# Turning the second context chunk of a streamed attention before its loop, and the later chunks three steps ahead instead of two

## The reference, cut to what matters

```python
x = x + xattn(layernorm(x), ctx)     # x: (2, 512, 512), ctx: (2, 8192, 512)
x = x + ssm(layernorm(x))            # long convolution through a Fourier transform
x = x + ffn(layernorm(x))            # 8 experts, each token takes the best one
# inside xattn
h = history @ hW.T + hb;  c = combined @ cW.T + cb
q = h @ qW.T + qb;  k = c @ kW.T + kb;  v = c @ vW.T + vb
attn = softmax(q @ k.T / sqrt(512))
out  = (attn @ v + q) @ oW.T + ob
```

## Time and profile before

| | |
|---|---|
| time, median of 3 runs | 1181.11 us (1179.37 to 1183.04) |
| the profiled execution, its own time | 1183.38 us |
| its span, first to last instruction | 1181.6 us |
| TensorE busy | 1097.0 us, 93% |
| TensorE weight loads busy | 887.9 us, 75% |
| VectorE busy | 925.3 us, 78% |
| ScalarE busy | 515.1 us, 44% |
| GpSimd busy | 483.9 us, 41% |
| mean granted TensorE clock | 0.966 |

### The profile page before, as it was taken

One profiled execution on the slowest core, in us unless ns is written; L12 is line 12 of the kernel. 1 busy time (PEld: TensorE's weight loads), 2 busy tenths in 40 slices (PEclk: granted clock), 3 DMA queues, 4 the chain that ended last, 5 costly groups with the idle time before them and its releaser, 6 DMA issues.

```text
span 1181.6 us, 16713 instructions
## 1 busy us (share of the span) xinstructions
PE 1097.0 (93%) x4945; PEld 887.9 (75%) x4945; DVE 925.3 (78%) x1979; ACT 515.1 (44%) x1091; POOL 483.9 (41%) x432
## 2 busy tenths in 40 slices
PE   7999989999999999999899999999999999565497
PEld 5787868788888888788678888888888888453365
DVE  7952688898888888865489889899898675978584
ACT  4221165565555555443444444444444422423261
POOL 4702154354454454212244444444443316452353
PEclk9999989999999999999999999999999999877599
DMA  8210579888678676423367868878866510117691
GB/s 280 96 57 36 89 195 201 201 200 199 178 194 197 178 192 164 125 72 86 75 174 184 202 173 194 200 174 195 199 178 180 155 37 1 71 38 248 234 330 59
DMA packets 202198, 184.36 MB, mean 156 GB/s; under 512 B 18160, under 2 KB 147216, under 8 KB 202146
## 3 DMA queue, kind: packets, MB, share of 16 engines
q1 hardware_dynamic: 180930, 141.26, 47.8%
q10 hardware_dynamic: 17856, 32.51, 7.9%
q0 software_dynamic: 3360, 9.97, 2.3%
HBM read 142.77 MB, written 42.73 MB: 157 GB/s over the span
## 4 chain that ended last, share of the span: by engine, by line
PE 75%; DVE 12%; issue 4%; POOL 4%; DMA 3%; ACT 1%; SPq 0%; POOLq 0%; ACTq 0%; DVEq 0%
PE bank L563 37%; PE bank L702 27%; PE bank L908 3%; PE bank L782 2%; PE bank L751 2%; PE bank L571 1%; DMA zT<-in_L_ffn_expert_w_dram 1%; DVE h L1450 1%; PE bank L597 1%; DVE probs L1450 1%; DMA spectra<-mixed,gather_rows 1%; POOL rows L1985 1%; DVE h L1326 1%; DMA stage<-in_L_xattn_hW_dram 1%; POOL hl_F L1860 1%
## 5 line engine op out<-in xcount | busy, mean ns | idle before, releaser
L563 PE MATMUL bank<-hl_C,hl_D 128*128 128x512 f32 x768 | 189.0, 396 | 11.7 <-POOL hl_C L1867 11.7
L702 PE MATMUL bank<-hl_F,probsT 128*128 128x512 f32 x768 | 190.7, 397 | 0.3 <-DVE probsT L1525 0.2
L702 PE MATMUL bank<-hl_A,probsT 128*128 128x512 f32 x768 | 190.3, 396 | 0.0
L563 PE MATMUL bank<-hl_B,hl_D 128*128 128x512 f32 x768 | 184.6, 390 | 0.3 <-POOL hl_B L1867 0.2
L563 PEld LDWEIGHTS bank<-hl_C,hl_D 128*128 128x128 f32 x768 | 146.7, 191 | 44.8 <-POOL hl_C L1867 12.5
L1053 ACT ACTIVATE probs<-bank,nbias 128x512 f32<-128x512 f32 x128 | 88.2, 689 | 208.3 <-DVE nbias L1513 208.3
L1860 POOL TENSOR_TENSOR hl_A<-stage,hl_A 128x512 fp32r<-128x512 f32 x64 | 84.7, 1324 | 215.9 <-ACT hl_A L1020 215.8
L1860 POOL TENSOR_TENSOR hl_F<-stage,hl_F 128x512 fp32r<-128x512 f32 x64 | 85.4, 1334 | 210.3 <-ACT hl_F L1020 210.3
L702 PEld LDWEIGHTS bank<-hl_F,probsT 128*128 128x128 f32 x768 | 144.0, 188 | 35.4 <-POOL hl_F L1860 0.6
L702 PEld LDWEIGHTS bank<-hl_A,probsT 128*128 128x128 f32 x768 | 144.2, 188 | 34.2
L563 PEld LDWEIGHTS bank<-hl_B,hl_D 128*128 128x128 f32 x768 | 143.9, 188 | 32.7 <-issue 1.2
(11 more groups left out here) (401 smaller groups left out, 1853.9 us busy)
## 6 DMA issues: line engine op xcount, KB each, us to landing
p_rows<-probs ACTq DMA_DIRECT2D x124, 256.0 KB, 3.2
stage<-in_ctx_dram SPq DMA_DIRECT2D x112, 256.0 KB, 3.6
spectra<-in_ctx_dram SPq DMA_DIRECT2D x64, 256.0 KB, 5.4
xb<-in_ctx_dram SPq DMA_DIRECT2D x64, 256.0 KB, 5.2
resid<-p_rows SPq DMA_DIRECT2D x248, 64.0 KB, 2.2
stage<-in_L_ffn_expert_w_dram SPq DMA_DIRECT2D x9, 1024.0 KB, 8.3
h<-p_rows SPq DMA_DIRECT2D x124, 64.0 KB, 2.1
obB<-p_rows SPq DMA_DIRECT2D x124, 64.0 KB, 2.3
```

The lines of the kernel that those rows point to most:

```text
L563: last = nc.tensor.matmul(dst, lhs[:, a, t, k * P:(k + 1) * P], rhs[:, c, t, :], start=(t == 0 and (a, c) == PASSES[0]), stop=(t == T - 1 ...
L702: last = nc.tensor.matmul(obank[u % 2][:], probsT[u % 2][:, a, j, :], nat[b][par][:, c, j, :], start=(j == 0 and (a, c) == PASSES[0]), sto ...
```

## The change

VectorE turns three blocks of chunk 1 ahead of the loop (`second_chunk`), not two. For the first attention they come before the four additions into `xb` (L1409), not behind them. In the loop it turns a block three steps before it was due by count, not two (`TURNED_AHEAD`), and in the second attention the turning stands ahead of the four spectral products of the step, not behind. ScalarE and GpSimd take blocks 0, 1 and 2 of chunk 1 in step 0 and block 3 in step 1 (`FIRST_BLOCKS`), and GpSimd takes these ahead of the natural tile of the step. SyncE loads all four quarters of a later chunk in the step in which it loaded the first two; before, the other two came a step later.

```diff
+FIRST_BLOCKS = ((0, 1, 2), (3,), (), ())
+TURNED_AHEAD = 3
@@ SyncE
                     if n % T == T - 1:
-                        next_squares(b, n // T + 3, (0, 1))
-                    elif n % T == 0:
-                        next_squares(b, n // T + 2, (2, 3))
+                        next_squares(b, n // T + 3)
...
-            def next_squares(b, c, rows_of):
-                if 2 < c < NCH:
+            def next_squares(b, c):
+                if c < NCH:
                     sp.wait_ge(cT_split, b * BLOCKS + T * (c - 2))
-                    for j in rows_of:
-                        load_square_rows(b, c, j)
+                    load_squares(b, c)
@@ ScalarE
-                            for dd in BLOCKS_OF_STEP[u % T]:
+                            for dd in blocks_of(u, first):
                                 context_block(t, u, dd)
@@ VectorE
+            def second_chunk(b):
+                dve.wait_ge(in_squares[b][1], 16 * T)
+                for dd in range(TURNED_AHEAD):
+                    nc.vector.transpose(squares[b][1][:, dd], squares[b][1][:, dd]).then_inc(cT_ready, 1)
...
                 nc.vector.tensor_copy(ubB[:], bank_of("ubias")[:]).then_inc(evacuated, 1)
+                second_chunk(0)
                 for k in range(T):
                     add_to_x(f"qo1.{k}", 1, k)
...
-                    par, dd = ((u + 2) // T + 1) % 2, (u + 2) % T
+                    par, dd = ((u + TURNED_AHEAD) // T + 1) % 2, (u + TURNED_AHEAD) % T
...
+                        if not (first and u < 2):
+                            row_sums(*back(t, u, 2))
+                        if not (last and u + TURNED_AHEAD >= T):
+                            next_square(t, u)
                         if not kernel_terms and u % 3 != 2 and u < 7:
                             output_products(u - u // 3, t, t * P, P, small_parts)
-                        if not (first and u < 2):
-                            row_sums(*back(t, u, 2))
-                        if not (last and u + 2 >= T):
-                            next_square(t, u)
...
-                dve.wait_ge(in_squares[b][1], 16 * T)
-                for dd in range(2):
-                    nc.vector.transpose(squares[b][1][:, dd], squares[b][1][:, dd]).then_inc(cT_ready, 1)
...
                 first_lo(1)
+                second_chunk(1)
@@ GpSimd
+                        if first and u < T:
+                            for dd in blocks_of(u, first):
+                                context_block(t, u, dd)
                         natural(t, u)
-                        if not (last and u >= T):
-                            for dd in BLOCKS_OF_STEP[u % T]:
+                        if not ((first and u < T) or (last and u >= T)):
+                            for dd in blocks_of(u, first):
                                 context_block(t, u, dd)
```

More of the change, by code:

```diff
@@ L345, in evacuated_by, with blocks_of @@
                 eng.wait_ge(evacuated, EVAC[name])
+        def blocks_of(u, first):
+            return FIRST_BLOCKS[u] if first and u < T else BLOCKS_OF_STEP[u % T]
         def back(t, u, n):
```

## The result

| | before | changed |
|---|---|---|
| median | 1180.24 us (1179.06 to 1183.04, 4 runs) | 1192.47 us (1190.89 to 1194.52, 4 runs) |
| ratio, 95% interval | | 1.0104 [1.0084, 1.0125] |
| first attention, loop start to the third last weighted sum | 355.5 us | 356.0 us |
| second attention, loop start to the first block of the tail | 370.1 us | 378.5 us |

The change costs 12.2 us. The forecast was a gain of 6; the result lies above its range. The two rows of stages are differences of two starts on TensorE in the profiled executions: 500.64 - 145.14 and 945.12 - 574.99 before, 500.53 - 144.52 and 953.42 - 574.92 after. So 8.4 us are lost inside the second attention.

What follows compares the result with a forecast made beforehand. TensorE was taken to bound the kernel, full in both loops, idle only at the starts. First attention +0.1, second -6.0, loops 0: -5.9 us, from the median 1181.11 to 1175; range 1172 to 1179.

Steps and rivals of the forecast that it cites:

- Chunk 1 ahead of the loop: Starts of both attentions: blocks split earlier, so step 5 starts 4.0 us earlier in the first, 7.3 in the second.
- the sum: Whole kernel: first attention +0.1 us, second -6.0, loops 0, together -5.9 us.
- The list of signs: What would show the forecast right or wrong, such as step 5 at 20.2 us behind the second loop's start.
- The first round of it: First chunks after the starts: four loads land at 177.8, chunk 2 is late, 3.3 us go back by step 8.
- Four loads together: Steady loops: four loads land in 8.5 us; zero cost taken, 1 us per chunk over 14 chunks as other end.
- the loads pace the loop: Rival, both loops: a landing beyond 8.4 us in the second attention costs time every chunk; 1186 us at 9.3; chance 0.26.
- in the same 2 to 3 us: Second attention's first rounds: late probabilities behind the four loads fall within the some 3 us VectorE is behind TensorE.
- loops 0: Steady loops of both attentions: neither gain nor loss, the second's VectorE wait just covered by 2.0 us of slack.

Runs made afterwards that it cites:

- e1: Changed kernel with the four spectral products again ahead of the step's row sums and turned block; 1182.03 us, ratio to before 1.0025.
- e4: Kernel before with the start part alone: three turned blocks, FIRST_BLOCKS, GpSimd's blocks first; loops as before; 1174.80 us, repeated 1173.97 us.
- e5: e4 with SyncE's four loads of squares in one group instead of two pairs; 1180.11 us, ratio to before 1.0005.
- e2: Kernel before with only the spectral products moved behind the row sums and turned block; 1195.59 us, ratio to before 1.0126.
- e6: e1 with SyncE's four loads of squares ahead of the probabilities' return instead of behind it; 1180.78 us, ratio to before 1.0017.
- e11: e4 with the products between the row sums and the turned block; 1174.71 us, ratio to before 0.9954.
- e10: e2 with GpSimd's splits of the second attention on an eighth of their elements; 1174.49 us, ratio to before 0.9944.

## Why the prediction was wrong

By steps of the prediction:

- *Chunk 1 ahead of the loop*: right, by the way that was forecast. The fourth maximum came at 159.32 for 160.1, tile 3 at 163.83 for 164.6, step 5 at 164.68 for 165.3 and, in the second attention, 6.5 us earlier for 7.3. Alone, with the loads in pairs, this part is worth 5.4 and 6.1 us in two measurements; the sum had 11.3 for it before anything went back, and 5.9 for the whole change. (The list of signs put 20.2 us behind the second loop's start; that is the first loop's figure, the working gives 17.8 and the trace 18.6: 593.48 - 574.92.)
- *The first round of it*: the landing was right to 0.2 us, the give-back too small. Counted from the loop's start, step 5 came 24.13 - 20.16 = 4.0 us earlier and step 8 0.4 later (185.46 - 144.52 against 185.71 - 145.14), so 4.3 us went back by step 8, where the term had 3.3. In the second attention the sum let 1.3 us go back. In e1, with the products at their old place, step 5 comes 5.8 us earlier, counted from the loop's start, and the whole attention is 0.2 us shorter (369.9 for 370.1), so 5.6 went back.
- *Four loads together*, the loop's squares: the landing was put at 8.5 us; bursts of the second attention landed 8.6 us (issued 734.61) and 9.6 us (758.76) after their first issue, so the bound of 8.4 of the rival "the loads pace the loop" was indeed passed, and VectorE waited in every second chunk, up to 3.0 us. But it cost the steady loop little: with the products ahead the same loads and the same three steps leave TensorE 1035 of 1041 matmuls between 660 and 900 us (e1). Their price is in the first rounds (245 for 262 between 600 and 660): they take back the start's gain and 1.8 us more (e1 against before; 7.2 against e4). The prediction did name the probabilities behind the four loads, and let their lateness fall "in the same 2 to 3 us"; the four loads at the new start cost 5.9 us (e5 against e4).
- **The failed step**: the term "loops 0", by the sentence "the block now stands ahead of the step's four products, of which the last two took 1.59 us and all four about 2". It carried the products' time of their old place to the new one. There the four took 4.16 us in the step shown. The zero stood on VectorE's 2.0 us of slack per chunk. By e2's rows the move alone adds (77.0 + 7.4 + 12.8) - (35.7 + 21.3 + 15.2) = 25.0 us in 240 (products, row sums, `dmax`), that is 2.3 in 22.16 us, past the slack (and some more per step, as e2's window holds one or two steps fewer). It costs 10.4 us in the changed kernel (1192.47 less e1's 1182.03) and 15.4 by itself. The prediction had the rule and the row for it, and applied them to the start alone.

Put together part by part, in this order, by the ratios times 1180: the start -5.3 (e4, 0.9955), the four loads +5.9 (e5, 1.0005), three steps ahead +2.4 (e1, 1.0025), the products behind the block +9.3 (1.0104), together +12.3 us. So even without the products the forecast 5.9 would not have come: start and four loads together are +0.6, which is the second term that failed, the give-back of the first rounds. The rival "slower: the loads pace the loop" gave the right sign and, at 1186, half the loss, by luck: its pacing of the steady loop is the 1.4 us that e1's 6 missing matmuls of 1041 are worth in 240. (By its own bound a landing of 9.3 would give 0.9 x 14 = 12.6 us, not 11.) Whether three steps ahead costs anything by itself stays open: e1, e5 and e6 don't tell it from nothing.

The version that beats both kernels is e4, at 1174.8 and 1174.0 us, or e11, its equal, at 1174.7.

## What to carry to other kernels

When an instruction is moved within an engine's order, its duration is not carried with it: read what the neighbouring engine does at the new place, and which of the two moved instructions can lie beside it. Here a turned block of 0.7 us put ahead of four products that took 0.86 us together made these take up to five times as long, and nearly twice on average (65.5 for 35.7 us). And take a change of several parts apart: a start worth 5 to 6 us was paid for with loads that only the third step ahead needed, and buried under a swap of two lines.

## What the runs showed of the hardware

Between 660 and 900 us the median `dmax`, a VectorE instruction on 128x1 elements with two SBUF inputs, took 149 to 150 ns in the kernel before, in the changed one, in e2 and in e10, but the longest 1147 ns in the kernel before, 836 in e2 and 154 in e10, with e2's order and short splits (means 345, 305 and 150). So even the smallest one can be held up for most of a split, and here it stands ahead of ScalarE's `alpha`. The splits themselves got hardly longer in the collisions: the median split of a block, hl_C and hl_B, took 1296 and 1293 ns before and 1324 and 1337 in the changed kernel, some 40 ns, where the means of the products beside them rose by 171 to 575. VectorE paid for nearly all of it.
